# A graph network kernel: order of the mask matmuls, of the last turned probabilities and of the second normalisation

## The reference, cut to what matters

```python
x = layernorm(x + L0(x, adj))      # 6 heads of 64: softmax(q k^T / 8 + mask) v, then @ Wf + bf
x = layernorm(x + L1(x, adj))
# L1, 12 heads of 32:
h = x @ W ; th = tanh(h)
attn = leaky_relu(th . w_src + (th . w_dst)^T, 0.2)      # per head, 128 x 128
attn = softmax(where(adj, attn, -999))
feat = elu(attn @ h + b)
gate = sigmoid(x @ H_w.T + H_b)
out  = gate * feat + (1 - gate) * x
```

## Time and profile before

| | |
|---|---|
| median of 3 runs | 1118.89 us (1118.72 to 1119.07) |
| the profiled execution | 1119.08 us |
| its span, first to last instruction | 1117.3 us |
| PE busy | 1053.9 us, 94% of the span |
| DVE, ACT, POOL busy | 888.8, 882.6, 766.3 us |
| granted TensorE clock, mean | 0.986 |

### The profile page before, as it was taken

How to read it: one execution, slowest core, us unless ns; L and a number is a source line. 1 busy time by engine, 2 the same in 40 slices (tenths; PEclk the granted TensorE clock), 3 DMA queues, 4 the chain that set the end, 5 groups by cost and what they waited for, 6 DMA issues and landing times.

```text
span 1117.3 us, 25374 instructions
## 1 busy us (share of the span) xinstructions
PE 1053.9 (94%) x8300; PEld 881.2 (79%) x8300; DVE 888.8 (80%) x1826; ACT 882.6 (79%) x3255; POOL 766.3 (69%) x911
## 2 busy tenths in 40 slices
PE   5889999999999999999999999999999999997773
PEld 5678888888888888888888888888888888886652
DVE  5457878888887888888788888878888887888875
ACT  3348888888888888888888888888888888888864
POOL 1467776776777677677767767776776777667652
PEclk9999999999999999999999999999999999999986
DMA  9101010020101002010100201010020101000000
GB/s 273 57 2 57 16 64 24 8 72 16 65 16 57 31 8 72 16 65 16 58 30 9 72 16 65 15 54 33 9 72 16 64 16 44 16 8 16 16 15 22
DMA packets 25892, 44.65 MB, mean 40 GB/s; under 512 B 2462, under 2 KB 23714, under 8 KB 25762
## 3 DMA queue, kind: packets, MB, share of 16 engines
q1 hardware_dynamic: 23234, 41.91, 11.0%
q10 hardware_dynamic: 2496, 1.12, 0.5%
q0 software_dynamic: 32, 0.00, 0.0%
HBM read 30.43 MB, written 12.58 MB: 39 GB/s over the span
## 4 chain that ended last, share of the span: by engine, by line
PE 57%; POOL 26%; issue 9%; DVE 5%; ACT 2%; DMA 1%; POOLq 0%; ACTq 0%; DVEq 0%
PE ps_b L253 13%; PE ps_d L253 13%; POOL z L963 9%; PE ps_a L253 7%; PE ps_d L460 5%; POOL xT_lo L911 5%; PE ps_a L382 4%; PE ps_s L362 3%; POOL p L990 3%; PE ps_s L354 2%; POOL s L955 2%; PE ps_c L470 2%; POOL thw L998 2%; POOL y L957 2%; PE ps_d L448 1%
## 5 line engine op out<-in xcount | busy, mean ns | idle before, releaser
L584 ACT ACTIVATE z<-z,s 128x128 f32<-128x128 f32 x768 | 297.3, 392 | 6.3 <-DVE s L791 6.3
L963 POOL TENSOR_TENSOR z<-z,mask 128x512 f32<-128x512 f32 x192 | 218.4, 1166 | 0.4 <-ACT z L678 0.4
L584 ACT ACTIVATION_READ_ACCUMULATOR z<-z,s 128x1 f32 x768 | 146.7, 191 | 0.0
L611 ACT ACTIVATE p<-ps_s,s 128x128 f32<-128x128 f32 x384 | 134.7, 378 | 11.4 <-DVE s L769 11.4
L990 POOL TENSOR_TENSOR p<-p,s 128x768 f32<-128x768 f32 x64 | 94.2, 1471 | 57.2 <-DVE s L797 57.2
L460 PE MATMUL ps_d<-ident,z 128*128 128x128 f32 x768 | 118.4, 277 | 10.5 <-ACT z L584 9.7
L952 POOL TENSOR_SCALAR s<-s 128x1 f32<-128x1 f32 x128 | 28.8, 225 | 141.5 <-DVE s L890 129.9
L998 POOL TENSOR_TENSOR thw<-th,w_sd 128x768 f32<-128x768 f32 x64 | 117.5, 1836 | 2.8 <-ACT th L634 2.8
L678 ACT ACTIVATE z<-ps_d 128x512 f32<-128x512 f32 x192 | 100.8, 598 | 20.9 <-PE ps_d L448 20.9
L460 PEld LDWEIGHTS ps_d<-ident,z 128*128 128x128 f32 x768 | 90.6, 142 | 18.2 <-ACT z L584 10.5
L791 DVE TENSOR_REDUCE s<-z 128x8 f32<-128x1024 f32 x64 | 77.9, 1216 | 26.4 <-POOL z L963 25.8
(11 more groups left out here) (156 smaller groups left out, 3398.0 us busy)
## 6 DMA issues: line engine op xcount, KB each, us to landing
x_cols<-in_xT_dram SPq DMA_DIRECT2D x16, 768.0 KB, 6.2
xb<-in_x_dram SPq DMA_DIRECT2D x16, 768.0 KB, 4.8
out_dram<-y SPq DMA_DIRECT2D x64, 192.0 KB, 1.9
z<-in_L_gnn_Wq_dram SPq DMA_DIRECT2D x1, 576.0 KB, 6.5
p1T<-in_L_gnn_Wk_dram SPq DMA_DIRECT2D x1, 576.0 KB, 8.8
qT<-in_L_gnn_Wv_dram SPq DMA_DIRECT2D x1, 576.0 KB, 11.2
kT<-in_L_gnn_Wf_dram SPq DMA_DIRECT2D x1, 576.0 KB, 13.3
z<-in_L_gnn_W_dram SPq DMA_DIRECT2D x1, 576.0 KB, 11.9
```

The costliest lines, as they stand in the source:

```text
L584: done = act.activation(z[:, a, :], z[:, a, :], ACT.Exp, bias=neg1[:, a:a + 1], accum_out=sum1[:, a:a + 1])
L611: last = act.activation(p0[:, o, i, :], ps_s[:, o, i * N:(i + 1) * N], ACT.Exp, bias=neg0[:, k:k + 1], accum_out=sum0[:, k:k + 1])
L963: pool.tensor_tensor(z[:, 4 * q:4 * q + 4, :], z[:, 4 * q:4 * q + 4, :], mask[:, t, :].unsqueeze(1).broadcast_to([P, 4, N]), ALU.add).then ...
```

## The change

On PE three things move inside a step. The mask matmuls of the next graph's scores (`scores_mask`, two of 384 columns) go from behind `logits` to behind the gate's bias matmul, ahead of Wf's product. Of Wf's three chunks only the first now stands ahead of `turn_sd` and the last group of `turn_p1`; chunks 1 and 2 follow them. Behind `logits` comes `apply_p1` directly. On POOL `second_norm` leaves the end of its step and runs one step later, behind the products `thw` and ahead of `first_norm`; the last one runs after the loop. For that `r1` and `mv1` have two buffers, and DVE's wait for `y` before it writes `r1` is for one graph earlier. The number of instructions that compute is the same, on every engine; DVE's and ACT's lists keep their order.

```diff
@@ -121,12 +121,12 @@
         p1T = sb("p1T", [P, H1, N])
         s2 = sb("s2", [P, 64])
         inv1, sum1 = s2[:, 0:12], s2[:, 40:52]
-        st1, mv1, ve1, rs1, nm1 = s2[:, 16:22], s2[:, 24:26], s2[:, 28:29], s2[:, 30:31], s2[:, 32:33]
+        st1, mv1, ve1, rs1, nm1 = s2[:, 16:22], (s2[:, 24:26], s2[:, 26:28]), s2[:, 28:29], s2[:, 30:31], s2[:, 32:33]
         fT = sb("fT", [P, C, N])
         ps_f = ps_c[:, 0:D].rearrange("p (a e) -> p a e", a=H1)
         ps_r = ps_c[:, 0:D]
         fe = sb("fe", [P, D])
-        r1 = sb("r1", [P, D])
+        r1 = sb("r1", [P, 2, D])
         y = sb("y", [P, 2, D])
 
         def staging(buffer):
@@ -134,7 +134,7 @@
 
         stage = [staging(z[:, :, :]), staging(p1T[:, :, :]), staging(qT[:, 1, :, :]), staging(kT[:, 1, :, :])]
         bf_in = th[:]
-        hb_row = r1[0:1, :]
+        hb_row = r1[0:1, 0, :]
         hb_rest = y[0:1, :, :]
         hb_split = gate[0:1, :, :].rearrange("p a d -> p (a d)").bitcast(BF16)[:, 0:3 * D].rearrange("p (a d) -> p a d", a=3)
         adj_u8 = x1[:].rearrange("p a j d -> p (a j d)")[:, 0:B * N // 4].bitcast(mybir.dt.uint8
@@ -513,18 +513,18 @@
                         turn_p1(tl - 1, gat, (1,))
                     if gat:
                         project_gate((2,))
-                    if att:
-                        project_out(ta, g, j, n, (0, 1))
-                    if gat:
-                        turn_sd(tl)
-                    if tail:
-                        turn_p1(tl - 1, gat, (2,))
-                    if att:
-                        project_out(ta, g, j, n, (2,))
-                    if gat:
-                        logits(tl)
                     if 0 <= ta and ta + 1 < B:
                         scores_mask(ta + 1)
+                    if att:
+                        project_out(ta, g, j, n, (0,))
+                    if gat:
+                        turn_sd(tl)
+                    if tail:
+                        turn_p1(tl - 1, gat, (2,))
+                    if att:
+                        project_out(ta, g, j, n, (1, 2))
+                    if gat:
+                        logits(tl)
                     if tail:
                         apply_p1(tl - 1, (j + 1) % 2, gat)
             pipeline(pe, iteration)
@@ -811,10 +811,10 @@
                         dve.scalar_tensor_tensor(ps_r, ps_r, -1.0, x1_, ALU.add, ALU.subtract
                                                  ).then_inc(S["tail_small"], 1)
                         dve.wait_ge(S["tail_small"], 3 * t2 + 2)
-                        if due(t2):
-                            dve.wait_ge(S["y_ready"], t2)
-
-                        dve.scalar_tensor_tensor(r1[:], gate[:, t2 % 3, :], 1.0, ps_r, ALU.add, ALU.mult
+                        if due(t2 - 1):
+                            dve.wait_ge(S["y_ready"], t2 - 1)
+
+                        dve.scalar_tensor_tensor(r1[:, t2 % 2, :], gate[:, t2 % 3, :], 1.0, ps_r, ALU.add, ALU.mult
                                                  ).then_inc(S["tail_small"], 1)
                     if att:
                         dve.wait_ge(S["p0_turned"], ta + 1)
@@ -883,11 +883,11 @@
                     if has_tail(n, j, 2):
                         t2 = tl - 2
                         dve.wait_ge(S["tail_small"], 3 * t2 + 3)
-                        dve.scalar_tensor_tensor(r1[:], r1[:], 0.25, x1_, ALU.mult, ALU.add).then_inc(S["r1_ready"], 1)
+                        dve.scalar_tensor_tensor(r1[:, t2 % 2, :], r1[:, t2 % 2, :], 0.25, x1_, ALU.mult, ALU.add).then_inc(S["r1_ready"], 1)
                         dve.wait_ge(S["r1_ready"], t2 + 1)
-                        dve.bn_stats(st1, r1[:]).then_inc(S["mv1_ready"], 1)
+                        dve.bn_stats(st1, r1[:, t2 % 2, :]).then_inc(S["mv1_ready"], 1)
                         dve.wait_ge(S["mv1_ready"], apart(dve, 2 * t2 + 1))
-                        dve.bn_aggr(mv1, st1).then_inc(S["mv1_ready"], 1)
+                        dve.bn_aggr(mv1[t2 % 2], st1).then_inc(S["mv1_ready"], 1)
                     if att:
 
                         dve.wait_ge(S["out_made"], ta + 1)
@@ -966,10 +966,12 @@
 
             def second_norm(t):
 
+                if due(t):
+                    pool.wait_ge(S["y_ready"], t)
                 pool.wait_ge(S["mv1_ready"], 2 * t + 2)
                 if t >= 2:
                     pool.wait_ge(S[f"y_stored_{t % 2}"], 16 * (t // 2))
-                normalise(r1[:], mv1, ve1, rs1, nm1, EPS / 4, y[:, t % 2, :], "ln1_small", 3 * t, "y_ready")
+                normalise(r1[:, t % 2, :], mv1[t % 2], ve1, rs1, nm1, EPS / 4, y[:, t % 2, :], "ln1_small", 3 * t, "y_ready")
 
             def first_norm(t):
 
@@ -997,6 +999,8 @@
                             pool.wait_ge(S["sd_ready"], tl)
                         pool.tensor_tensor(thw[:], th[:].unsqueeze(1).broadcast_to([P, 2, D]), w_sd[:], ALU.mult
                                            ).then_inc(S["thw_ready"], 1)
+                    if has_tail(n, j, 3):
+                        second_norm(tl - 3)
                     if 0 <= ta - 1 < B:
                         first_norm(ta - 1)
                     if ta == 0:
@@ -1013,9 +1017,8 @@
                     if n == 0 and j == 3:
                         xb_with_bias(g, par, slice(0, 2))
                         xb_with_bias(g, par, slice(2, 4))
-                    if has_tail(n, j, 2):
-                        second_norm(tl - 2)
             pipeline(pool, iteration)
+            second_norm(B - 1)
 
 
 def kernel(**inputs):
```

More of the change, by code:

```diff
@@ L515, in iteration @@
                         project_gate((2,))
+                    if 0 <= ta and ta + 1 < B:
+                        scores_mask(ta + 1)
                     if att:
-                        project_out(ta, g, j, n, (0, 1))
+                        project_out(ta, g, j, n, (0,))
                     if gat:
@@ L522, in iteration @@
                     if att:
-                        project_out(ta, g, j, n, (2,))
+                        project_out(ta, g, j, n, (1, 2))
                     if gat:
                         logits(tl)
-                    if 0 <= ta and ta + 1 < B:
-                        scores_mask(ta + 1)
                     if tail:
```

## The result

| | us |
|---|---|
| kernel before, median of 20 runs | 1119.82 (1116.71 to 1124.42) |
| changed kernel, median of 20 runs | 1123.42 (1120.38 to 1129.18) |
| ratio | 1.0040, 95% interval 1.0028 to 1.0051 |
| profiled execution of the change | 1126.55, span 1124.7, granted clock 0.983 |

The change makes the kernel slower by 0.4%, 3.6 us; 1124.1 was forecast.

A forecast was written before the change was run, and what follows sets the result against it. PE's list, busy 94%, was taken to bound the middle steps, with ACT's chain to fT only 0.14 us from a wait. 12.0 + 0.3 - 5.8 - 1.3 - 0.6 + 0.6 = +5.2 on 1119.08, less 0.2: 1124.1 us; range 1120 to 1131.

The forecast's parts named there:

- The mask matmuls and the logits, +12.0: PE, graphs 1 to 60: masks delay logits and ACT's relus, so fT's transposes wait; +0.20 us per step, +12.0 us.
- The +0.3 for graph 61: PE, graph 61: no mask left to move, but the later Wf chunks still push its logits back; about +0.3 us.
- rival 1: PE's list alone sets the step, each 0.25 us shorter; faster, 1096 us; chance 10%.
- The wait for p, -5.8: PE behind x_lo: y no longer delays z's mask on POOL, so 13 waits of 0.44 for p go; -5.8 us.
- The gate, left out: PE's L460: the gate, ended 1.06 after the bias matmul plus 0.06 signal, is just in time for transposes at 1.15.
- The sd parts, +0.6: DVE beside POOL: x's later normalisation overlaps the sd parts, done at 0.95 to 1.0; 0.01 per step, +0.6 us.
- the second rival: POOL's x normalisation holds DVE's sd parts, turn_sd 0.18 to 0.22 later; 45 steps cost 9, 1133 us; chance 12%.
- the mark that the prediction named for the rival: In the changed profile, L434 waiting for sd_parts would show that x's normalisation holds up the sd parts.
- The end, -1.3: Last graph: DVE's wait of 1.38 for z's mask, held up by y on POOL, goes; about -1.3 us.
- the first steps, -0.6: PE, graphs 0 and 1: masks fill 0.35 of each wait of about 1.3 ahead of Wf's product; -0.6 us.
- The clock (rival 3): The added wait of 0.4 drops PE's clock in the four steps that wait most; +6, 1130 us; chance 8%.

The follow-up runs named there:

- e4: The changed kernel with turn_x1 moved ahead of turn_f on PE; 1095.12 us, 0.9791 of the kernel before, and 1095.28 us when run again.
- e2: PE's part alone: the change's PE order, with POOL's order and the single r1 of the kernel before; 1124.07 us, ratio 1.0052.
- e3: The changed kernel with Wf's chunks split as before, two ahead of turn_sd, so only the masks move on PE; 1119.36 us, ratio 0.9995.
- e1: POOL's part alone: second_norm behind thw with both buffers, PE's order of the kernel before; 1108.27 us, ratio 0.9902.
- the second profile: The changed kernel run and profiled again without an edit, as a control; 1121.57 us, ratio 1.0027 to the kernel before.
- e9: e4 with second_norm between z's mask and p for j above 0 in steps with next-group projections, otherwise behind thw; 1091.73 us, ratio 0.9768.

## Why the prediction was right, and where its terms were off

The time, 1124.1 for 1123.42, was met in part by luck. The median of the kernel before was 0.9 us higher over the 20 runs than over the three of the forecast, and the difference, +5.2 forecast and +3.6 measured, holds errors of 2 to 4 us that cancel. By the steps of the prediction:

**The mask matmuls and the logits, +12.0.** The mechanism is shown. L478 waits for fT in each of 64 graphs where it waited in 4, logits come at 2.8, apply_p1 0.32 behind, and ACT's chain is the 2.43 that was worked out. e4 confirms it from the other side: fill the wait, and the loss is gone. The size was 0.16 per step (e2) or 0.17 (e3 less e1) and not 0.20. In e2 and e4 the logits start at 2.75, not 2.82. I had carried the masks' whole 0.35 over from turn_sd to the logits. The list from turn_sd to the logits is 665.39 - 663.66 = 1.73, where three more matmuls of 0.173 on the 646.14 - 644.89 = 1.25 of the earlier trace rows would make 1.77, and turn_sd itself comes at 1.02 and not 1.04. 60 x 0.16 is 9.6 us, 2.4 less than forecast. The +0.3 for graph 61 can't be read: its step took 15.70 before and 14.67 and 15.11 in the change, at granted clocks of 0.83, 0.93 and 0.89. Nothing in any run reads as PE's list setting the step while the wait is there (rival 1).

**The wait for p, -5.8.** It goes as told, in all 13 steps, and the four long waits stay. The size was wrong: 13 steps by 0.62 to 0.65 are the -8.2 of e1's middle, where 5.8 was forecast. The term took the idle time as printed for the price. The price is what the starts are apart, less what they are apart without a wait.

**The gate, left out.** The prediction has the gate ready 1.06 after the bias matmul and L460 "just in time". That holds for three of four kinds of step. Behind an x_lo the gate is ready at 1.14 to 1.15 in every kernel here; it cost nothing at the old place of L460 (1.34), and at the new one it holds L460, the logits and fT's transposes back. In e2, where no sd part is held, the transposes start at 5.27 in these steps and at 5.18 in the others. That is 13 x 0.09 = +1.2 us.

**The sd parts, +0.6.** This term was mis-sized, and the second rival was a part of the truth. Against e1 the change is 13.5 us longer in its middle (12.4 in the second profile). The masks make 56 x 0.155 = 8.7 of it and the gate 1.2. The rest, 3.6 (2.5), is the hold; counted step by step it is 3.6 (2.4). In the three other kinds the steps are 0.02 to 0.06 longer than e2's, 2.4 us (2.3) together. Behind an x_lo, where the first parts are later, it depends on L865. In 7 of the 13 steps of the change's first profile it was held as shown above: the last part was done at 1.21 and the step took 16.03. In the other 6, and in 12 of 13 in the second profile, it ran free, the last part was done at 1.03 and the step took 15.87, which the gate would allow anyway. That is 0.16 for each step with L865 held, 7 of them against 1. The prediction said the part is held to POOL's end plus 0.03 and is done at 0.95 to 1.0; it was done at 0.98 to 1.02, and it did not look at the steps behind an x_lo by themselves. PEld's wait for sd_parts, 14.6 us in 58 cases, is the mark that the prediction named for the rival. It shows in the view of the weight loads, in PE's own only twice. That the hold costs at all needs both halves of the change. In e1 the parts are as late, at 1.01 to 1.05, and turn_sd is not due before 1.22; in e2 turn_sd is due early and the parts are done at 0.75, or 0.84 behind an x_lo. This is why the halves, -8.2 in the middle for POOL's and +7.0 for PE's, don't give the whole, +5.2 (4.1 in the second profile): 13 x 0.25 = 3.3 us of masks and gate were hidden behind p's wait in e2, which went from 0.44 to 0.19, and the hold comes on top.

The Trainium skill, page "SBUF — State Buffer", section "SBUF: two separate sides", would have the earlier of the two instructions hold the ports throughout. The held L865 agrees with it, but it cost 0.16 in 7 steps and not the 0.2 in 45 of the second rival; in the other kinds the hold costs 0.02 to 0.06. Two instructions shown at the end of this text don't agree.

**The end, -1.3, and the first steps, -0.6.** DVE's idle time of 1.38 at the end went, and 1.38 came off the last stretch in the first profile. In that profile the step ahead, at the lower clock, took it back. From the first bias matmul to the second it is 17.04 instead of 17.25, -0.2; the rest of -0.6 can't be told from the scatter of the start. The waits ahead of Wf's product there did shrink, from 1.3 each to 0.6 and 0.9 (0.9 and 0.9 in the second profile), but the next wait for p grew from 0.81 to 1.16.

**The clock (rival 3).** No wider fall in the middle: the steps there repeat within 0.05 with few exceptions, and the new waits of 0.38 left the granted clock of the middle at 1.00. In the four last steps of the layer the waits changed little, and 57 to 61 lasts 59.72 for 59.58. It falls in the steps behind them, as it did before.

With the sizes as measured the middle is 8.7 for the masks, -8.2 for p, 1.2 for the gate and 3.6 (2.4) for the hold, together +5.3 (4.1), where the profiles have 5.2 and 4.1. With +0.1 from 57 to 61, about -1.3 for the end and -0.2 for the first step this gives +3.9 and +2.7. The runs say +3.6 and, the second time, +2.4 (1121.57 less 1119.19), with intervals from 3.1 to 5.7 and from 1.2 to 4.7.

What stays open: why the hold starts so late (below), why the gate is later behind an x_lo, and what decides whether the last steps run at the lower clock. No run changes any of them alone.

## What to carry to other kernels

When work is moved ahead on the engine that is always busy, follow also what it pushes back. Here it was the start of another engine's chain whose end the busy engine needs, with only 0.14 us to spare; the repair is to put independent work between the chain and its consumer, and e4 turned a loss of 0.4% into a gain of 2.1%. A wait's price is read from the starts of the two instructions with and without it, since the printed idle time (0.44) was only two thirds of what the wait cost (0.65). And a change of several parts is priced by steps of one kind, as two halves may each be harmless and meet in one place.

## What the runs showed of the hardware

A DVE instruction on 24 columns beside POOL's normalisation (0.66) is not held from the moment that POOL's begins. In the kernel before, a cast that started 0.08 after POOL's took 0.20. In e9, with POOL's at 616.42, a subtraction that started 0.11 after it took 0.18, and the cast after that was held to 617.12, 0.03 after POOL's end:

```profile
616.42 0.67 POOL L957 TENSOR_SCALAR x<-r,s 128x384 f32<-128x384 f32 x1
616.53 0.18 DVE L865 TENSOR_TENSOR sd_rest<-sd,sd_parts 128x24 f32<-128x24 f32 x1
616.74 0.38 DVE L868 CAST sd_parts<-sd_rest 128x24 bf16<-128x24 f32 x1
```

In the change one that started 0.15 after it was held. By the rule named above, the first two should have been held too (the cast as well, since the same cast was held in e9). The twelve profiles of this case agree on where the hold begins: none of the casts and subtractions that started within 0.14 of such an instruction was held, and each of the 477 that started 0.146 or more behind it was, to 0.03 or 0.04 after its end. Between the two it went either way. In the change, L865 starts 0.13 to 0.15 after POOL's instruction behind an x_lo, so a hundredth of a microsecond decides whether it is held and whether the step takes 15.87 or 16.03.

The masks' two matmuls cost 0.32 to 0.35 among others of their tile, about as forecast (turn_sd starts at 1.54 in e3 and at 1.22 in e1), and 0.45 between the logits, whose tile has 32 rows, and apply_p1 (0.91 less 0.46). Whether the change of tile is the reason no run shows. The 0.46 held 0.14 of waiting by the third logits matmul for its p1T: in the change the three take 0.39 and apply_p1 follows after 0.32.
